# A six-stage transformer kernel: the second attention's weight split, border writes and norms are done at other places

## The chip, the cores and the metric

The kernel runs on one core of a Trainium2 chip. The core has five engines with a queue of instructions each: TensorE (PE), VectorE (DVE), ScalarE (ACT), GpSimd (POOL) and SyncE (SP, which here only issues DMAs). They run beside each other and wait for each other through semaphores. The metric is the device time of one execution in microseconds (us).

## The reference

The input x has 8 sequences of 256 tokens with 128 features (2048 rows). Six blocks follow each other, each on a layer norm of x and each added to x. The change concerns the fifth:

```python
x = x + 0.5 * _L0_ffn_ref(_layernorm(x), ...)    # f0: 64 experts, top 8
x = x + _L0_attn_ref(_layernorm(x), ...)         # a0
x = x + 0.5 * _L0_ffn_ref(_layernorm(x), ...)    # g0
x = x + 0.5 * _L1_ffn_ref(_layernorm(x), ...)    # f1: 8 experts, top 2
x = x + _L1_attn_ref(_layernorm(x), ...)         # a1
x = x + 0.5 * _L1_ffn_ref(_layernorm(x), ...)    # g1

# _L1_attn_ref: 16 heads of 64, causal, with a relative bias that depends on the query
Q = X @ Wq + bq;  K = X @ Wk;  V = X @ Wv        # 128 -> 16*64
R = X @ Wr + br                                  # 128 -> 16*10
extra[h,t,p] = sum_n R[h,t,n] * b_nd[n, t-p]     # only where p <= t
logits = Q K^T / 8 + extra, masked;  W = softmax(logits)
out = (W V) @ Wproj + bproj
```

## The kernel before, in words

Six stages f0, a0, g0, f1, a1, g1 run one after the other. Each is a set of five programs, one for each engine, written out by hand; what an engine does next is the order of its own program, and no scheduler changes it. At the end of a stage every engine passes a common barrier (`stage_end`), so nothing of a1 starts before f1 is done. x stays in SBUF from the first stage to the last.

**Stage a1 (`attention_one`)** works on a sequence (batch) at a time. Its products need more precision than one pass gives, so each operand is cut into a high part and a rest (`high_part`, `rest_part`) and a product is three matmuls (`matmul_by_parts`, lines 211 to 213). A batch's products come in 21 *pieces*, each of which fills one PSUM bank and is copied out by DVE or ACT (`store_piece`; those with odd number by ACT):

- R: X@Wr for both halves of the heads, six matmuls; DVE adds the bias and writes `RT`.
- G0 to G7: `RT` times the bias table `bnd`, one matmul each, of 40 partitions by 512 (in the trace two records each). The copy goes to `G`.
- QK0 to QK7: the transposed Q and K of two heads, six matmuls.
- V0 to V3: three matmuls of 512 columns.

G is written to a DRAM buffer `z` in rows three spans wide, whose two outer spans hold a large constant; read back with a stride one shorter than a row (line 1836, to `X0`, `X1`), it comes out shifted row by row: the bias by key, with the mask in place. Four pieces of G make half of a batch's heads (`c` is 0 or 1): two DMAs write them, and once these have landed two DMAs read them back.

**The start of a1 before the change.** DVE takes the statistics of all 16 tiles of 128 rows, then normalises them one by one (line 161, `a_xn`); PE turns each (line 167) into banks 0 to 3, and ACT copies each bank to `a_xnT` (line 180). Meanwhile SP loads the raw weights (lines 1795 to 1807), into the space of `X1[0]`, and then writes the borders of `z` from a tile `pad` with six DMAs (line 1814). After `a_xnT` ACT makes the high parts of the weights (line 2040), DVE the rests (line 202), and DVE then adds `bproj` to all of x (line 2093). POOL waits for all of `a_xnT` and then splits the first two batches' columns (`split`, lines 197 and 202, tiles `a_xs_high`, `a_xs_rest`). Only when DVE is through (`pe.wait_ge(prep, 2)`, `pe.wait_ge(w_rest, 4)`) does PE begin the first batch's pieces. They alternate between banks 5 and 6, in the order of the table `STEPS`:

```python
STEPS = ([("R", 0), ("QK", 0)], [("G", 0), ("G", 1), ("QK", 1)], [("G", 2), ("G", 3), ("QK", 2)], ...
```

A piece waits until its bank has been read, and a step's pair of G waits for both banks. Only after all 21 pieces does the main loop begin: 64 steps of two heads, scores (line 1932), logits on DVE (2107, 2109), exponentials on ACT (2049, 2051), normalising (1869, 1870), turning (1944), values (1964), with the next batch's pieces in between, and the projection (1974). In the loop POOL only splits later batches.

**Stage f1 (`mixture_one`)** is the one ahead. Its POOL program sends 32 groups of rows to their experts' slots by indirect DMAs (line 378); PE waits for them and for the gathered rows (line 347), and then does 39 passes (434, 444, 453). DVE has by then added the output bias (569) and copied the first three passes' weights (589).

## Time and profile before

| | us |
|---|---|
| median of 3 runs | 1273.78 (1270.94 to 1274.09) |
| profiled execution: its own time | 1271.9 |
| profiled execution: span, first to last instruction | 1269.9 |
| stage a1, first DVE instruction to g1's | 741.73 to about 1098 |
| in it: start of the first scores on PE | 792.00 |
| PE busy, of the span | 988.7 (78%) |
| DVE busy, of the span | 820.0 (65%) |
| POOL busy, of the span | 276.7 (22%) |

The times in the profile are microseconds from the first instruction. A busy share over the whole span says little here, as the six stages have different limits; the stage's own stretch is to be read. [...]

### The profile page before, as it was taken

To read this page: it belongs to the slowest core of one execution; us is meant where nothing else is said; L and a number is where in the kernel's file an instruction comes from. 1 tells how busy PE (TensorE), PEld (TensorE's weight loads), DVE (VectorE), ACT (ScalarE), POOL (GpSimd) and SP (SyncE) were. 2 spreads that over 40 slices of the span, in tenths; PEclk is the share of its full clock that TensorE was granted. 3 is DMA by queue.
4 is the path that set the end of the run, shared out by engine and by line. 5 is a ranking of instruction groups with operands and counts; after the bars stand their busy time and mean duration, and the time that the engine had idled before them with its cause. 6 is when DMAs were issued, how large, how long until landed. Compare 5 with 4: busy or idle time off the path is not lost.

```text
span 1269.9 us, 25097 instructions
## 1 busy us (share of the span) xinstructions
PE 988.7 (78%) x7978; PEld 739.0 (58%) x7978; DVE 820.0 (65%) x2678; ACT 572.9 (45%) x1503; POOL 276.7 (22%) x313
## 2 busy tenths in 40 slices
PE   4599867999996599894299717899999999634992
PEld 3256755666764255683179714566677666522992
DVE  5875887477876875787235482767776767570554
ACT  3103552356564102472045412777777777511551
POOL 2201136223201201202734410000000000055552
PEclk9799885589998699896599956999999999856997
DMA  8004000000006103009140178544345542464113
GB/s 226 1 0 114 0 15 0 1 1 2 1 2 160 34 0 100 13 1 227 52 107 29 29 256 241 164 120 135 116 133 167 143 123 68 77 174 118 33 32 105
DMA packets 131421, 105.39 MB, mean 83 GB/s; under 512 B 7987, under 2 KB 118107, under 8 KB 131316
## 3 DMA queue, kind: packets, MB, share of 16 engines
q1 hardware_dynamic: 126772, 95.55, 27.3%
q0 software_dynamic: 4544, 8.54, 2.1%
q8 instruction: 55, 0.90, 0.3%
q14 instruction: 50, 0.41, 0.1%
HBM read 66.14 MB, written 38.83 MB: 83 GB/s over the span
## 4 chain that ended last, share of the span: by engine, by line
PE 57%; DVE 22%; issue 8%; POOL 5%; ACT 3%; DMA 2%; DVEq 1%; POOLq 0%; SPq 0%; PEld 0%; ACTq 0%; PEldq 0%
PE psum L823 6%; PE psum L444 5%; PE psum L908 5%; PE psum L453 4%; PE psum L1433 3%; PE psum L211 3%; PE psum L1932 3%; PE psum L1482 3%; PE psum L1944 2%; PE psum L1974 2%; POOL f_slots_dram L378 2%; POOL g_slots_dram L378 2%; PE psum L1964 2%; PE psum L167 2%; PE psum L895 2%
## 5 line engine op out<-in xcount | busy, mean ns | idle before, releaser
L1613 DVE TENSOR_REDUCE a_negmax<-psum 128x2 f32<-128x512 f32 x128 | 84.9, 688 | 44.3 <-PE psum L1433 43.5
L1050 DVE TENSOR_TENSOR g_S<-g_place,g_number 128x512 bf16<-128x512 f32 (+1 forms) x116 | 76.8, 703 | 16.4 <-PEq L818 6.0
L1562 ACT ACTIVATE a_PT<-psum 128x1024 f32<-128x1024 f32 x64 | 65.4, 1022 | 34.9 <-PE psum L1465 34.6
L482 ACT ACTIVATE f_hT<-psum,f_tile_bias 128x128 f32<-128x128 f32 x156 | 44.5, 368 | 77.0 <-PE psum L444 77.0
L482 ACT ACTIVATE g_hT<-psum,g_tile_bias 128x128 f32<-128x128 f32 x156 | 44.5, 368 | 73.6 <-PE psum L444 73.6
L1050 DVE TENSOR_TENSOR f_S<-f_place,f_number 128x512 bf16<-128x512 f32 (+1 forms) x100 | 66.2, 704 | 14.9 <-PEq L818 6.2
L2049 ACT ACTIVATE a_pr<-a_L,a_least 128x128 f32<-128x128 f32 x128 | 50.8, 397 | 54.4 <-DVE a_least L2109 54.4
L1433 PE MATMUL psum<-a_turned 24*128 24x256 f32 x256 | 63.5, 377 | 5.7 <-DVE a_negmax L1613 5.6
L2051 ACT ACTIVATE a_pr<-a_L,a_least 128x256 f32<-128x256 f32 x128 | 63.6, 497 | 0.0
L1932 PE MATMUL psum<-a_KT,a_Q 64*128 64x128 f32 (+1 forms) x512 | 59.3, 350 | 1.4 <-DVE a_least L2109 1.4
L1459 PE MATMUL psum<-a_turned 24*128 24x256 f32 x256 | 57.3, 370 | 0.0
L2059 ACT ACTIVATE a_PT<-psum 128x384 f32<-128x384 f32 x128 | 55.6, 490 | 1.7 <-PE psum L1944 1.6
L1433 PEld LDWEIGHTS psum<-a_turned 24*128 24x128 f32 x256 | 42.6, 220 | 22.5 <-DVE a_negmax L1613 11.2
L1964 PE MATMUL psum<-a_PT,a_V 128*64 128x256 f32 (+1 forms) x512 | 55.5, 339 | 0.0
L1944 PE MATMUL psum<-ident,a_pr 128*128 128x128 f32 x384 | 52.9, 274 | 2.8 <-DVE a_pr L1870 2.5
L1964 PEld LDWEIGHTS psum<-a_PT,a_V 128*64 128x64 f32 x512 | 31.1, 136 | 40.9 <-issue 16.8
L197 POOL CAST a_xs_high<-a_xnT 128x256 fp32r<-128x256 f32 x8 | 4.3, 540 | 228.8 <-PE psum L213 219.0
L2109 DVE CUSTOM_DVE_ANT_0 a_L<-psum,a_X 128x256 f32<-128x256 f32 x128 | 53.8, 420 | 0.0
L384 POOL DMA_INDIRECT g_back_dram<-g_y,g_xin x39 | 43.3, 1109 | 43.7 <-DVE g_y L583 41.2
L589 DVE COPY f_wt<-f_w 128x1024 f32 x39 | 29.2, 749 | 35.9 <-PE psum L453 25.9
L384 POOL DMA_INDIRECT f_back_dram<-f_y,f_xin x39 | 40.8, 1047 | 48.8 <-DVE f_y L583 47.1
L589 DVE COPY g_wt<-g_w 128x1024 f32 x39 | 27.9, 720 | 34.9 <-PE psum L453 31.4
(527 smaller groups left out, 2875.9 us busy)
## 6 DMA issues: line engine op xcount, KB each, us to landing
a_z<-a_G SPq DMA_DIRECT2D x32, 512.0 KB, 3.2
a_X<-a_z SPq DMA_DIRECT2D x16, 1024.0 KB, 7.2
a_X<-a_z SPq DMA_DIRECT2D x16, 512.0 KB, 3.9
f_wgu<-in_gate_up SPq DMA_DIRECT2D x16, 384.0 KB, 6.6
...
a_z<-a_pad SPq DMA_DIRECT2D x6, 1024.0 KB, 8.6
...
```

The source lines that it names most:

```text
L384: pool.indirect_dma_start(back_dram[:, :], bass.IndirectOffsetOnAxis(ap=xin[:, i, P:P + 1].bitcast(I32), axis=0), y[i % YBUF][:, :], None, ...
L444: last = pe.matmul(bank[i % 2][:, P * c:P * c + P], wt[i % WBUF][:, P * c:P * c + P], xT[:, i % 2, :], start=True, stop=True)
L482: act.activation(hT[:, i % 2, c, :], bank[i % 2][:, P * c:P * c + P], ACT.Relu, bias=tile_bias[:, c, i:i + 1]).then_inc(relu_done, 1)
L823: pe.matmul(bank[k], xpart[:, i, ds(t, 1), :].rearrange("p t n -> p (t n)"), S[:, k, :], start=False, stop=False, skip_group_check=True)
L1050: return dve.tensor_tensor(S[:, slot, :].rearrange("p (t e n) -> p t e n", t=1, n=CAPACITY), bcast(place[:, ds(t, 1), CE * k:CE * k + CE], ...
L1433: last = pe.matmul(bank[h % 2][:, SEQ * t:SEQ * t + SEQ], q[rows, g, P * t:P * t + P].bitcast(F32R), k[rows, g, :].bitcast(F32R), start=Tr ...
L1562: act.activation(PT[m % 4][:, :, :, :].rearrange("p j t n -> p j (t n)"), core.psum[:, 2 + 2 * (u % 2):4 + 2 * (u % 2), :], ACT.Exp, scale ...
L1613: dve.tensor_reduce(negmax[:, :, h], bank[h % 2].rearrange("p (t n) -> p t n", n=SEQ), AX.X, ALU.max, negate=True).then_inc(max_done, 1)
L1932: last = pe.matmul(out, Q[s][rows, c, queries], KT[s][rows, c, keys], start=True, stop=True)
L1944: last = pe.transpose(bank[2 + i][:, P * j:P * j + P], pr[:, n % SLOTS, P * j:P * j + P], core.ident[:, :])
L1964: last = pe.matmul(o[D1 * i:D1 * i + D1, queries], V[s][:, kt, D1 * h:D1 * h + D1], PT[:, (2 * m + i) % TSLOTS, keys], start=(kt == 0), st ...
L2051: act.activation(pr[:, o, P:3 * P], L[:, o, P:3 * P], ACT.Exp, bias=least[:, o, 1:2], scale=-1.0, accum_out=sums[:, o, 1:2]).then_inc(p_re ...
```

## The change

- A new class `Early` holds a1's weights in high and rest parts, its bias tables and `z`. Its loads (SP), zero fills (POOL), high parts (ACT) and rests (DVE) are issued in stage f1: the loads behind f1's own weights, the fills at the head of POOL's program, the high parts ahead of f1's first relu, the rests between line 569 and line 589 of before. The raw weights have their own space.
- `pad` is filled at the head of a0 on POOL, and the six border DMAs are issued by SP in a0.
- In a1 DVE normalises only the first quarter (4 tiles); POOL does the other three. PE turns the first quarter, and the other three in between the first batch's pieces; ACT takes them likewise.
- The first batch's pieces use banks 5, 6, 7 and 4 in turn, in a new order, `FIRST`. Later batches are as before.
- `bproj` is added to x by POOL, a batch at a time, behind `split`; DVE's add of the projection waits for it.

```diff
+class Early:
+    def wait_split(self, eng):
+        eng.wait_ge(self.loaded, self.LOADS * 16)
+        eng.wait_ge(self.w_rest, len(self.cuts))
+        eng.wait_ge(self.prepared, 1)
+    def gpsimd(self, pool):
+        for m in (self.bnd[:, :, :], self.br[:, :], *(m[:, :, :, :] for m in self.wr)):
+            pool.memset(m, 0.0).then_inc(self.zeroed, 1)
+    def sync(self, sp):
...
+        for raw, m in zip(self.raw, ("Wq", "Wk", "Wv")):
+            sp.dma_start(raw[:, :], w[m]).then_inc(self.loaded, 16)
...
+    def scalar(self, act):
+        act.wait_ge(self.loaded, self.LOADS * 16)
+        act.wait_ge(self.zeroed, 4)
+        for raw, parts in self.cuts:
+            high_part(lambda out, in_: act.activation(out, in_, ACT.Copy), parts[0], raw).then_inc(self.w_high, 1)
+    def vector(self, dve):
+        dve.wait_ge(self.loaded, self.LOADS * 16)
+        dve.tensor_scalar(self.bq[:, 1, :], ...).then_inc(self.prepared, 1)
+        for i, (raw, parts) in enumerate(self.cuts):
+            dve.wait_ge(self.w_high, i + 1)
+            rest_part(dve, parts[1], raw, parts[0]).then_inc(self.w_rest, 1)
 def attention_one(core, name, ctx, w):
+    PIECE_BANKS = (5, 6, 7, 4)
+    FIRST = ([("R", 0)] + [("G", j) for j in range(4)] + [("QK", 0), ("QK", 1)] + [("G", j) for j in range(4, 8)]
+             + [("QK", 2), ("V", 0), ("V", 1), ("V", 2), ("V", 3)] + [("QK", j) for j in range(3, 8)])
     def gpsimd(pool):
-        pool.wait_ge(ln.xnT_ready, 4)
+        pool.wait_ge(ln.xn_ready, 4)
+        ln.normalise(pool, 1)
         split(0)
         split(1)
+        ln.normalise(pool, 2)
+        ln.normalise(pool, 3)
+        pool.wait_ge(early.prepared, 1)
+        add_bias(0)
+        add_bias(1)
         for b in range(BATCH):
             if b + 2 < BATCH:
                 split(b + 2)
+                add_bias(b + 2)
     def tensor(pe):
-        ln.tensor(pe)
-        pe.wait_ge(loaded, LOADS * 16)
-        pe.wait_ge(ln.xnT_ready, 4)
+        ln.turn_quarter(pe, 0)
+        early.wait_split(pe)
...
-        pe.wait_ge(prep, 2)
-        pe.wait_ge(w_rest, 4)
-        for u in range(len(STEPS)):
-            tables(0, u)
-            projections(0, u)
+        pe.wait_ge(zeroed, 1)
+        for n, k in enumerate(FIRST):
+            piece(0, k)
+            if n in (5, 8, 12):
+                ln.turn_quarter(pe, (5, 8, 12).index(n) + 1)
     def vector(dve):
-        ln.vector(dve)
-        dve.wait_ge(loaded, LOADS * 16)
-        dve.tensor_scalar(bq[:, 1, :], bq[:, 0, :], -RSCALE, None, ALU.mult).then_inc(prep, 1)
-        for i, (raw, parts) in enumerate(cuts):
-            dve.wait_ge(w_high, i + 1)
-            rest_part(dve, parts[1], raw, parts[0]).then_inc(w_rest, 1)
-        dve.wait_ge(ln.xn_ready, TILES)
-        dve.tensor_tensor(core.x[:, :, :], core.x[:, :, :],
-                          bp_row[:, :].unsqueeze(1).to_broadcast([P, TILES, P]), ALU.add).then_inc(prep, 1)
+        ln.statistics(dve)
+        ln.normalise(dve, 0)
```

PE at the start of a1, before the change: all 16 tiles are turned, then R (its six matmuls are two rounds of the first three rows), QK0 (`wq`, `wk`) and the first pair of G (`a_bnd,a_RT`), after which the same seven rows come again for QK1 and G2, G3, and so on.

```order
L167 MATMUL psum<-ident,a_xn 128x128 x16
L211 MATMUL psum<-a_xs_high,a_wr_rest 104x256
L212 MATMUL psum<-a_xs_rest,a_wr_high 104x256
L213 MATMUL psum<-a_xs_high,a_wr_high 104x256
...
L211 MATMUL psum<-a_xs_high,a_wq_rest 128x256
L212 MATMUL psum<-a_xs_rest,a_wq_high 128x256
L213 MATMUL psum<-a_xs_high,a_wq_high 128x256
L211 MATMUL psum<-a_xs_high,a_wk_rest 128x256
L212 MATMUL psum<-a_xs_rest,a_wk_high 128x256
L213 MATMUL psum<-a_xs_high,a_wk_high 128x256
L1896 MATMUL psum<-a_bnd,a_RT 128x512 x2
```

PE at the same place now (other line numbers; `early_` names the tiles of the new class):

```order
L278 MATMUL psum<-ident,a_xn 128x128 x4
L322 MATMUL psum<-a_xs_high,early_wr_rest 104x256
L323 MATMUL psum<-a_xs_rest,early_wr_high 104x256
L324 MATMUL psum<-a_xs_high,early_wr_high 104x256
...
L1985 MATMUL psum<-early_bnd,a_RT 128x512 x4
L322 MATMUL psum<-a_xs_high,early_wq_rest 128x256
L323 MATMUL psum<-a_xs_rest,early_wq_high 128x256
L324 MATMUL psum<-a_xs_high,early_wq_high 128x256
L322 MATMUL psum<-a_xs_high,early_wk_rest 128x256
L323 MATMUL psum<-a_xs_rest,early_wk_high 128x256
L324 MATMUL psum<-a_xs_high,early_wk_high 128x256
L278 MATMUL psum<-ident,a_xn 128x128 x4
```

Twelve of the sixteen turned tiles have moved from ahead of R to between the pieces, and four matmuls of G stand together in front of QK0.

DVE from the norms of a1 to its first piece, before:

```order
L161 TENSOR_SCALAR a_xn<-x,a_mean_var,a_rstd 128x128 x16
L2087 TENSOR_SCALAR a_bq<-a_bq 128x8
L202 TENSOR_TENSOR a_wr_rest<-a_X_0,a_wr_high 128x4x40
L202 TENSOR_TENSOR a_wq_rest<-a_X_0,a_wq_high 128x1024
L202 TENSOR_TENSOR a_wk_rest<-a_X_0,a_wk_high 128x1024
L202 TENSOR_TENSOR a_wv_rest<-a_X_0,a_wv_high 128x1024
L2093 TENSOR_TENSOR x<-x,a_bp_row 128x2048
L2010 TENSOR_SCALAR a_RT<-psum,a_br 104x256 x2
```

DVE there now:

```order
L272 TENSOR_SCALAR a_xn<-x,a_mean_var,a_rstd 128x128 x4
L2105 TENSOR_SCALAR a_RT<-psum,early_br 104x256 x2
L2113 COPY a_G<-psum 128x512 x2
L2118 TENSOR_SCALAR a_Q<-psum,early_bq 128x256
L2119 COPY a_KT<-psum 128x256
```

POOL there now, where before it had only the pairs of lines 197 and 202:

```order
L272 TENSOR_SCALAR a_xn<-x,a_mean_var,a_rstd 128x128 x4
L308 CAST a_xs_high<-a_xnT 128x256
L313 TENSOR_TENSOR a_xs_rest<-a_xnT,a_xs_high 128x256
L308 CAST a_xs_high<-a_xnT 128x256
L313 TENSOR_TENSOR a_xs_rest<-a_xnT,a_xs_high 128x256
L272 TENSOR_SCALAR a_xn<-x,a_mean_var,a_rstd 128x128 x8
L1936 TENSOR_TENSOR x<-x,early_bp_row 128x256 x2
```

Between the norms of the first quarter and R, DVE has lost five instructions; the norms of the second quarter now stand ahead of POOL's first split.

## Rows read from the trace of the kernel before

**Rows 1.** Windows: busy us and instructions of each engine, PEclk, DMA share, GB/s

```profile
748.00:752.50 4.50, 4.23 (x16) 2.90 (x16) 3.93 (x16) 1.79 (x4) 0.00 (x0) 0.50 0.98 268
763.80:783.70 19.90, 13.26 (x34) 6.20 (x34) 4.40 (x8) 3.88 (x8) 0.00 (x0) 0.50 0.81 237
783.70:787.20 3.50, 3.49 (x15) 3.25 (x15) 0.82 (x2) 0.52 (x2) 0.00 (x0) 0.55 0.67 201
787.20:792.00 4.80, 4.60 (x24) 3.07 (x22) 2.20 (x4) 1.57 (x4) 0.00 (x0) 1.00 0.92 282
```

**Rows 2.** Timeline, start of a1: start us, length us, engine, instruction, idle before

```profile
747.74 4.19 DVE L161 TENSOR_SCALAR a_xn<-x,a_mean_var,a_rstd 128x128 f32<-128x128 f32 x16
...
756.78 1.74 DVE L202 TENSOR_TENSOR a_wv_rest<-a_X,a_wv_high 128x1024 fp32r<-128x1024 f32 x1
758.44 2.28 DVE L2093 TENSOR_TENSOR x<-x,a_bp_row 128x2048 f32<-128x2048 f32 x1
...
760.93 0.51 PE L211 MATMUL psum<-a_xs_high,a_wr_rest 128*104 128x256 f32 x1 [8.47 <-DVE x L2093]
```

**Rows 3.** POOL: line 1325 (ns, min/median/max), and timeline of the first split

```profile
L1325 POOL TENSOR_SCALAR a_diag<-ident,a_wl x3: 597/597/598, 183.6 to 184.8; 128x128 f32<-128x128 f32 x3
...
753.16 0.40 POOL L197 CAST a_xs_high<-a_xnT 128x256 fp32r<-128x256 f32 x1 [9.79 <-ACT a_xnT L180]
753.64 0.72 POOL L202 TENSOR_TENSOR a_xs_rest<-a_xnT,a_xs_high 128x256 fp32r<-128x256 f32 x1
```

**Rows 4.** Timeline, first batch's pieces on PE, with DVE's copy of R

```profile
762.31 0.42 PE L211 MATMUL psum<-a_xs_high,a_wq_rest 128*128 128x256 f32 x1
...
762.62 0.88 DVE L2010 TENSOR_SCALAR a_RT<-psum,a_br 104x256 f32<-104x256 f32 x2 [1.90 <-PE psum L213]
...
763.38 0.42 PE L213 MATMUL psum<-a_xs_high,a_wk_high 128*128 128x256 f32 x1
...
764.75 2.08 PE L1896 MATMUL psum<-a_bnd,a_RT 40*128 40x512 f32 x4 [0.96 <-DVE a_KT L2024]
...
786.44 0.59 PE L211 MATMUL psum<-a_wv_high,a_xs_rest 128*128 128x512 f32 x1
786.87 0.40 PE L212 MATMUL psum<-a_wv_rest,a_xs_high 128*128 128x512 f32 x1
...
792.00 0.93 PE L1932 MATMUL psum<-a_KT,a_Q 64*128 64x128 f32 x8
...
795.76 1.13 PE L1896 MATMUL psum<-a_bnd,a_RT 40*128 40x512 f32 x4 [0.39 <-DVE a_KT L2024]
```

**Rows 5.** Windows and timeline: another rise of PEclk, and a long low stretch

```profile
204.00:260.00 56.00, 52.95 (x266) 38.10 (x267) 28.18 (x53) 16.18 (x22) 14.20 (x17) 0.50 0.00 1
...
1104.15 4.09 PE L167 MATMUL psum<-ident,g_rows 128*128 128x128 f32 x16 [7.09 <-DVE g_rows L161]
...
1107.00:1108.50 1.50, 1.50 (x11) 1.17 (x10) 0.85 (x4) 0.82 (x2) 0.00 (x0) 0.76 1.23 226
```

**Rows 6.** Lines of ACT, 741 to 793: busy us, mean ns, idle before

```profile
L2005 ACT ACTIVATE a_G<-psum 128x512 f32<-128x512 f32 x4 | 2.4, 597 | 20.1 <-PE psum L1896 20.1
```

**Rows 7.** DMA of 740 to 800: KB each, median us to landing

```profile
a_z<-a_G SPq DMA_DIRECT2D x5, 512.0 KB, 2.9
a_X<-a_z SPq DMA_DIRECT2D x2, 1024.0 KB, 6.8
```

**Rows 8.** Timeline of f1: DVE's weight copies, POOL's scatter, DVE's next work

```profile
608.99 0.97 POOL L378 DMA_INDIRECT f_slots_dram<-f_rows,f_slot  x1 [0.30 <-issue]
...
609.96 2.19 DVE L589 COPY f_wt<-f_w 128x1024 f32 x3
610.26 1.27 POOL L378 DMA_INDIRECT f_slots_dram<-f_rows,f_slot  x1 [0.30 <-issue]
611.84 1.16 POOL L378 DMA_INDIRECT f_slots_dram<-f_rows,f_slot  x1 [0.30 <-issue]
...
641.32 0.49 DVE L577 COPY f_xT<-psum 128x128 f32<-128x128 f32 x2 [29.17 <-PE psum L434]
```

More of the change, by code:

```diff
@@ L35 @@
 FC1 = F1 // P
+H1, D1, NB1, SPAN = 16, 64, 10, 128
+CH = H1 // 2
+RH = 8
+ZW = 3 * SPAN
+MASKED = 1e9
 class Chain:
@@ L138, in vector, with statistics @@
     def vector(self, dve):
+        self.statistics(dve)
+        for q in range(4):
+            self.normalise(dve, q)
+    def statistics(self, dve):
         c = Chain(self.chain)
@@ L159, in vector, with normalise @@
         step(dve.tensor_tensor(rstd, rstd, t, ALU.mult))
-        for t in range(TILES):
-            dve.tensor_scalar(self.xn[:, t, :], x[:, t, :], self.mean_var[:, t, 0:1], self.rstd[:, t:t + 1],
+    def normalise(self, eng, q):
+        x = self.core.x
+        for t in range(4 * q, 4 * q + 4):
+            eng.tensor_scalar(self.xn[:, t, :], x[:, t, :], self.mean_var[:, t, 0:1], self.rstd[:, t:t + 1],
                               ALU.subtract, ALU.mult).then_inc(self.xn_ready, 1)
@@ L329, in mixture_one @@
     back_loaded = [sem(f"back_loaded{i}") for i in range(4)]
+    early = core.early if name == "f1" else None
     def sync(sp):
@@ L355, in gpsimd @@
     def gpsimd(pool):
+        if early:
+            early.gpsimd(pool)
         pool.memset(empty[:, 0:P], 0.0).then_inc(empty_filled, 1)
@@ L1753, in attention_one @@
     piece_done = core.sem(f"{name}_piece_done")
-    piece_read = [core.sem(f"{name}_piece_read{i}") for i in range(2)]
+    piece_read = [core.sem(f"{name}_piece_read{i}") for i in range(len(PIECE_BANKS))]
     z_written = [core.sem(f"{name}_z_written{c}") for c in range(2)]
@@ L1880, in piece @@
             _, i, used = at(b, kind)
-            out = bank[5 + i]
+            out = bank[PIECE_BANKS[i]]
             if which == "R":
@@ L1925, in scores @@
             wait_piece(pe, b, "QK", c)
+            if not n:
+                pe.wait_ge(ln.xnT_ready, 4)
             if n:
@@ L2067, in take_values @@
             act.activation(AT[:, c, :], bank[4 + 3 * (c % 2)][:, 0:SEQ], ACT.Copy).then_inc(aT_ready, 1)
-        for u in range(len(STEPS)):
-            pieces_stored(act, True, 0, u)
+        for n, k in enumerate(FIRST):
+            if by_act(k):
+                store_piece(act, True, 0, k)
+            if n in (6, 10, 14):
+                ln.take_quarter(act, (6, 10, 14).index(n) + 1)
         for n in range(BATCH * CH + VLAG):
@@ L2122, in add @@
             dve.wait_ge(out_done, b + 1)
+            dve.wait_ge(x_biased, b + 1)
             xb = core.x[:, 2 * b:2 * b + 2, :]
             dve.tensor_tensor(xb, xb, bank[7][:, 0:SEQ].rearrange("p (t n) -> p t n", n=P), ALU.add).then_inc(out_added, 1)
-        for u in range(len(STEPS)):
-            pieces_stored(dve, False, 0, u)
+        for k in FIRST:
+            if not by_act(k):
+                store_piece(dve, False, 0, k)
         for n in range(BATCH * CH):
@@ L2149, in build @@
         stage_done = core.sem("stage_done")
+        core.early = Early(core)
         made, sems, held = [], [], []
@@ L2163, in build @@
         out_dram = out.rearrange("(t p) d -> p t d", p=P)
+        names = [name for name, _ in stages]
         def stage_end(eng, n):
@@ L2174, in _ @@
                 st["sync"](sp)
+                if names[n] == "a0":
+                    core.early.write_pads(sp)
                 if n:
@@ L2185, in _ @@
             for n, st in enumerate(made):
+                if names[n] == "a0":
+                    core.early.fill_pad(pool)
                 st["gpsimd"](pool)
```

169 lines of the change are left out of this document (99 added, 70 removed).

## The prediction

> **What bounds the kernel now.** The stages stand behind barriers, so I read only the stage that is changed and the two that take over its work. First the windows by stage part [rows 1]: from 748.0 to 792.0 the granted clock is 0.50 until 787 and PE is busy for two thirds of it. The reader is to see that this stretch, ahead of the first scores at 792.00 [rows 4], has no engine that is full. Then the timeline of the stage's start [rows 2]: R, the first piece, begins at 760.93 and had waited 8.47 us for DVE, which was splitting weights and adding bproj from 752 to 760.7. Third the timeline of the pieces [rows 4]: from 760.93 to 792.00 are 31.1 us, in which PE works at the lower clock and pauses at each pair of G (0.96 us ahead of the first), because two banks must both be read. The rest of a1 is a loop of 64 steps whose instructions the change leaves as they are, but for POOL's adds.
>
> **The start of the stage.** DVE's four norms of the first quarter end at 747.74 + 4.19/4 = 748.8 [rows 2]. R now needs, on POOL, four norms, the cast (0.40) and the rest (0.72 with a gap of 0.08) [rows 3]. The trace has no norm on POOL. The nearest row is a tensor_scalar of the same 128x128 with one factor, 0.597 us; a norm has two. Bounds: 0.40, the cast of twice the size, and 0.72, the two-input operation of twice the size [rows 3]; so four cost 1.6 to 2.9 us. I take 4 x 0.60 = 2.4. Then 748.8 + 2.4 + 1.2 = 752.4, and with 0.1 for the signal R starts at 752.5. That is 8.4 us earlier than 760.93. The first quarter's turning and its copy on ACT run beside POOL's norms: they were going at 749.4 to 750.0 before too, ahead of 751.2.
>
> POOL's other splits and norms: second split until 753.6, eight norms until 758.4, each well ahead of the turning that needs it (below: 760.6 at the earliest). The two first bias adds, about 0.7 us each, follow; the remaining six lie in the loop, in which POOL had only the splits. Their consumer on DVE is a whole batch later. I cost them at nothing; if DVE's SBUF work is held up by them, 8 x 0.7 = 5.6 us is the most it could cost in 300 us of loop, and DVE has pauses there.
>
> [...]
>
> **The pieces.** Durations at the lower clock [rows 4]: R 762.31 - 760.93 = 1.4; QK five steps in 1.07, so six matmuls 1.28; a pair of G 2.08, so 1.04 each; V 3 x 0.43 = 1.29. A quarter's turning is 4.23/4 = 1.06 [rows 1]. A pair of G takes 1.13 at the full clock [rows 4], a factor of 0.54, which I use for all.
> - R from 752.5 to 753.9. G0 waits for DVE's copy of R: 763.50 + 0.1 against 762.31, a gap of 1.3. G0 starts at 755.2.
> - From there PE has, all at the lower clock, 8 x 1.04 (G) + 8 x 1.28 (QK) + 4 x 1.29 (V) + 3 x 1.06 (turning) = 8.3 + 10.2 + 5.2 + 3.2 = 26.9 us of work.
> - No more waits: a bank comes round after three other pieces, at least 1.7 us even at the full clock, and a copy is 0.60 on ACT for G [rows 6], 0.9 for QK, each engine having only half of them (some 8 us on DVE, 10 us on ACT with its three quarters). What hides them is PE's own queue; with two banks again it would be the pauses of [rows 4].
> - When does the clock rise? In the trace it rose at 786.85 (0.55 in a window of 3.5 us is a tenth of it at 1.00), 3.1 us into the first stretch without a pause and without G [rows 1], and at 1107.7, 3.6 us into 16 turned tiles [rows 5]. It did not rise in 16 tiles at 748.2 to 752.5, nor in the 19.9 us in which G and QK took turns [rows 1], nor from 204 to 260, where PE was busy for 53 of 56 us with matmuls of which most use 24 partitions [rows 5]. In the new order matmuls of G (40 partitions) stand at 755.2 to 759.4, and again, with turning between, at 763.0 to 768.2. From there on, QK2, V and QK3 to QK7, all have 128 partitions. I put the rise 3.4 us (mean of 3.1 and 3.6) behind 768.2, at 771.6.
> - Until then 16.4 of the 26.9 us are done; the other 10.5 take 10.5 x 0.54 = 5.7. First scores at 777.3 instead of 792.0: 14.7 us earlier, 8.4 of them from the start, 6.3 from pauses and clock.
> - Late next are the X tiles, which DVE's first logits need. G3 ends at 759.4, its copy at 760.2; write 2.9, two reads with the larger 6.8 us after its issue [rows 7], about 1 for issuing: 770.9. This is 6 us ahead of need. SP has no longer the borders to write in front of them.
> - ACT loads its exponential table only behind the copy of QK7, which is now the last piece; before it was V3. I add 0.2.
>
> **Borders in a0.** Six writes of 1 MB and one small fill of POOL. The DMAs stand behind a0's loads on SP, whose program there ends with them; a0 ran with idle DMA (share 0.00 [rows 5]). Nothing waits but SP. Cost 0, at most 0.3 for the fill.
>
> **Split in f1.** Loads of 2.2 MB behind f1's weights, ACT 3.5 us ahead of the first relu, DVE three rests of at most 1.74 [rows 2] and a small one of 0.4, 5.6 us at most and about 4.9 as the longest had POOL beside it, behind the bias additions. DVE is then idle for 29.17 us until 641 [rows 8], as POOL scatters rows; it hides DVE and ACT. But POOL's scatter is what ends last there. Beside DVE's 2.19 us of weight copies two of its instructions took 1.27 and 1.16 instead of 0.97 us [rows 8], a loss of 0.5. The new 4.9 us of DVE could cost between 0 and 0.5 x 4.9/2.2 = 1.1; I take 0.7. [...] POOL's four fills at the head, 1.4 us, delay the emptying of the slots, with 5 us to spare.
>
> **Sum.** -14.7 + 0.2 + 0.7 = -13.8 us. On the profiled execution's own time of 1271.9: 1258.1. The median of the three runs is 1.9 above that execution, the lowest 1.0 below; I add 0.9, half of it: 1259.
>
> **The rivals.**
> - *The clock rises in the first dense stretch.* For it: from 755.2 PE has no pause at all, which it never had before. Against: 4.2 of the first 7.8 us are G. With the rise at 759 to 763, 3.8 to 7.8 us are done low, and the scores start at 771.7 to 773.5, the X tiles being there at 770.9. That is 4 to 5.5 us better, 1254. [...]
> - *It does not rise before the scores.* Scores at 755.2 + 26.9 = 782.1, a gain of 9.9, less 0.9: 1263, or 1264 with the half offset. POOL's norms at their upper bound would add 0.5.
> - *Slower: the low clock goes on into the loop.* Now the loop has always run at 1.00, as the last pieces raised it. A long low spell in a busy PE exists, 56 us in a0 [rows 5]. The loop's PE is busy to about nine tenths; the same 56 us at a factor 0.54 to 0.6 would lose 22 to 25 us against a gain of 9: 1286. It decides from about 20 us of low loop on. Against it: 13.9 us of matmuls of 128 partitions stand directly ahead of the loop, where 3.1 and 3.6 were enough.
> - *The gain is not there because something is waited for elsewhere*: POOL's scatter slowed more, or the X tiles late by the traffic of f1 or a0. Price 3 to 8 us: 1262 to 1267.
>
> **Chances.** Forecast 0.50, early rise 0.26, no rise before the scores 0.13, low loop 0.04, held up elsewhere 0.07. The range from 1250 to 1267 takes in all but the low loop, and bounds for POOL's norms and the runs' own spread of 3 us. 0.3% is 3.8 us, about what a measurement of this kernel can tell from no change: only the slow loop is above 1277.6, and a part of the last case could be within. Faster 0.93, same 0.03, slower 0.04.
>
> **What would show it.** R's first matmul 11 us behind the stage's first DVE instruction, not 19; POOL's norms near 0.6 us; no pause above 0.3 us on PE between G0 and the scores; PEclk 0.50 while G stands between, 1.00 from 16 us behind G0; first scores 35.6 us into the stage (50.3 before). In f1, the stretch of the scatter longer by under 1.1 us. It is wrong if the pauses remain, if DVE's first logits wait for a DMA, or if the loop takes longer than before.

## The result

| | before | after |
|---|---|---|
| median, us | 1273.93 (4 runs, 1270.94 to 1274.53) | 1256.20 (4 runs, 1252.07 to 1260.92) |
| profiled execution: time, span | 1271.9, 1269.9 | 1252.09, 1250.3 |
| stage a1 in it | 355.9 | 339.5 |
| R behind the stage's start | 19.2 | 11.68 |
| first scores behind the stage's start | 50.27 | 32.15 |
| first scores to g1 | 305.7 | 307.3 |
| the five other stages | 906.5 | 903.4 |

The ratio is 0.9883, with a 95% interval of 0.9844 to 0.9922: 1.2% faster. The same kernel, run again in more rounds as the experiment `again`, had 1258.02 (6 runs, 1241.21 to 1260.18) and 0.9854 [0.9802, 0.9905]. Ratios are taken from fast runs alone, and two of these six count as slow (1260.18, which is the profiled one, and 1259.84), so the ratio isn't that of the two medians. Stage times are taken from one stage's first statistics instruction on DVE to the next one's. Of the 19.6 us by which the two profiled spans differ, 16.4 are a1. The other 3.1 can't be put down to the change: a0 took 213.7 us before and 202.8 after, f0 and g0 each 4 us more, and later kernels show 202 or 211 to 214 us for a0 with the same code, by how long its low clock lasts (from 204 until 238 in `after`, from 196 until 261 in `before`).

The windows of the changed kernel, start of a1 (busy us and count of PE, PE's weight loads, DVE, ACT and POOL, then PEclk, the granted clock of TensorE as a share of its full speed, DMA share, GB/s); they answer to [rows 1]:

```profile
752.80:756.60 3.80, 3.71 (x8) 1.18 (x8) 0.73 (x2) 0.60 (x1) 3.80 (x6) 0.50 0.00 0
756.60:760.20 3.60, 3.60 (x18) 3.49 (x16) 1.50 (x3) 0.60 (x1) 2.37 (x4) 0.50 0.97 290
760.20:763.10 2.90, 2.90 (x13) 1.12 (x12) 0.69 (x1) 1.80 (x4) 0.00 (x0) 0.94 0.13 23
763.10:770.80 7.70, 7.70 (x54) 6.98 (x52) 4.19 (x9) 4.27 (x9) 0.00 (x0) 1.00 1.05 318
777.50:781.50 4.00, 3.93 (x22) 3.55 (x24) 1.35 (x7) 2.85 (x9) 0.00 (x0) 0.57 0.50 153
```

PE is full from G0 (752.89) to the scores. The clock is back at 1.00 at about 760.6, 7.7 us behind G0 and not 16 us. The last window is new: some us into the loop the clock falls again, for 3.4 us (0.57 over 4 us); before, the whole loop ran at 1.00.

The timeline of the changed kernel, rows that answer to [rows 2 to 4] (start us, length us, engine, instruction, idle before):

```profile
744.68 1.11 DVE L272 TENSOR_SCALAR a_xn<-x,a_mean_var,a_rstd 128x128 f32<-128x128 f32 x4
745.90 3.14 POOL L272 TENSOR_SCALAR a_xn<-x,a_mean_var,a_rstd 128x128 f32<-128x128 f32 x4 [6.74 <-DVE a_xn L272]
749.00 0.39 POOL L308 CAST a_xs_high<-a_xnT 128x256 fp32r<-128x256 f32 x1
749.48 0.72 POOL L313 TENSOR_TENSOR a_xs_rest<-a_xnT,a_xs_high 128x256 fp32r<-128x256 f32 x1
750.35 0.51 PE L322 MATMUL psum<-a_xs_high,early_wr_rest 128*104 128x256 f32 x1 [4.03 <-POOL a_xs_rest L313]
...
770.82 0.93 PE L2024 MATMUL psum<-a_KT,a_Q 64*128 64x128 f32 x8
771.78 0.29 DVE L2192 CUSTOM_DVE_ANT_0 a_L<-psum,a_X 128x128 f32<-128x128 f32 x1 [0.74 <-PE psum L2024]
...
774.59 1.13 PE L1985 MATMUL psum<-early_bnd,a_RT 40*128 40x512 f32 x4 [0.39 <-DVE a_KT L2119]
777.57 0.54 PE L322 MATMUL psum<-a_xs_high,early_wq_rest 128*128 128x256 f32 x1 [1.85 <-DVE a_G L2113]
```

R waits for POOL now, for 4.03 us where it waited 8.47 for DVE. A norm on POOL is 0.785 us (3.14/4). The first logits wait for PE, not for a DMA. The pause of 1.85 us behind the first G of the loop stood in the kernel before as well, without a fall of the clock.

f1 in the changed kernel, DVE and POOL; it answers to [rows 8]:

```profile
626.31 0.69 DVE L688 TENSOR_TENSOR x<-x,psum 128x512 f32<-128x512 f32 x1 [10.52 <-remote]
...
627.22 1.22 DVE L313 TENSOR_TENSOR early_wq_rest<-early_raw_wq,early_wq_high 128x1024 fp32r<-128x1024 f32 x1
628.06 1.23 POOL L495 DMA_INDIRECT f_slots_dram<-f_rows,f_slot  x1 [0.30 <-issue]
...
629.59 1.97 POOL L495 DMA_INDIRECT f_slots_dram<-f_rows,f_slot  x1 [0.30 <-issue]
630.63 2.04 DVE L710 COPY f_wt<-f_w 128x1024 f32 x3
631.86 1.05 POOL L495 DMA_INDIRECT f_slots_dram<-f_rows,f_slot  x1 [0.30 <-issue]
```

The scatter's instructions lengthen from 0.97 to 1.23, 1.97 and 1.05 us beside DVE's rests and copies. From its first to its last it takes 41.31 us (595.74 to 637.05), before 40.54. DVE's last bias addition came at 626.31; before it was at 609.21. This returns below.

### The profile page after: what moved, and what is told of

The parts are those of the page before. It is cut to its first block, busy times and chain, and to the rows that moved or that the text cites. A ratio compares the mean times of both kernels' runs of the same rounds, so it can differ in the third digit from the quotient of the medians.

```text
span 1250.3 us, 25112 instructions
## 1 busy us (share of the span) xinstructions
PE 982.0 (79%) x7978; PEld 738.3 (59%) x7978; DVE 812.6 (65%) x2665; ACT 573.8 (46%) x1503; POOL 296.7 (24%) x333
## 4 chain that ended last, share of the span: by engine, by line
PE 56%; DVE 21%; issue 11%; SPq 5%; ACT 3%; DMA 2%; POOL 2%; DVEq 0%; PEld 0%; POOLq 0%; ACTq 0%; PEldq 0%
PE psum L561 6%; PE psum L944 6%; PE psum L570 5%; PE psum L1029 5%; PE psum L1554 3%; PE psum L1603 3%; PE psum L322 2%; PE psum L2024 2%; PE psum L2069 2%; PE psum L2036 2%; DVE a_L L2194 2%; PE psum L1016 2%; SPq L454 1%; PE psum L324 1%; PE psum L323 1%
## 5 line engine op out<-in xcount | busy, mean ns | idle before, releaser
L1554 PE MATMUL psum<-a_turned 24*128 24x256 f32 x256 | 59.6, 355 | 6.6 <-DVE a_negmax L1734 6.4
L501 POOL DMA_INDIRECT f_back_dram<-f_y,f_xin x39 | 44.8, 1148 | 41.0 <-DVE f_y L704 40.0
L1580 PE MATMUL psum<-a_turned 24*128 24x256 f32 x256 | 53.0, 349 | 0.0
L1554 PEld LDWEIGHTS psum<-a_turned 24*128 24x128 f32 x256 | 39.3, 203 | 21.8 <-DVE a_negmax L1734 11.0
```

The costliest lines, as they stand in the source:

```text
L501: pool.indirect_dma_start(back_dram[:, :], bass.IndirectOffsetOnAxis(ap=xin[:, i, P:P + 1].bitcast(I32), axis=0), y[i % YBUF][:, :], None, ...
L1554: last = pe.matmul(bank[h % 2][:, SEQ * t:SEQ * t + SEQ], q[rows, g, P * t:P * t + P].bitcast(F32R), k[rows, g, :].bitcast(F32R), start=Tr ...
```

## The experiments

Lengths in us from each profile. "Low in the loop" is the time at 0.50 behind the first scores, from the granted clock. Where no count of runs stands, it is one run (four for `before` and `after`); the kernel before, timed beside them, had medians of 1271.1, 1274.5, 1275.4 and 1271.1.

| run | time | R | scores | scores to g1 | a1 | low in the loop | f1 |
|---|---|---|---|---|---|---|---|
| before | 1273.93 | 19.2 | 50.27 | 305.7 | 355.9 | 0 | 170.2 |
| after | 1256.20 | 11.68 | 32.15 | 307.3 | 339.5 | 3.4 | 170.2 |
| again | 1258.02 (6) | 11.67 | 31.63 | 311.8 | 343.4 | 17.1 | 167.5 |
| g_first | 1259.39 | 11.67 | 35.19 | 308.1 | 343.3 | 6.8 | 167.7 |
| two_banks | 1255.23 | 11.67 | 41.5 | 307.2 | 348.7 | 3.4 | 170.5 |
| split_late | 1264.64 | 16.29 | 37.09 | 307.2 | 344.3 | 3.4 | 168.0 |
| quarter_dve | 1250.44 (5) | 9.70 | 29.65 | 311.7 | 341.4 | 17.1 | 170.1 |
| warm | 1254.53 | 11.67 | 31.16 | 307.1 | 338.2 | 3.4 | 167.4 |
| pads_late | 1258.38 | 11.67 | 31.79 | 312.7 | 344.5 | 10.2 | 167.1 |
| loop_fill | 1251.56 (4) | 11.67 | 31.58 | 305.8 | 337.4 | 0 | 167.5 |
| warm_rt | 1254.18 | 11.68 | 27.95 | 307.5 | 335.4 | 3.4 | 173.4 |
| both | 1259.92 (6) | 9.70 | 30.21 | 305.5 | 335.8 | 0 | 174.9 |
| everything | 1255.97 (6) | 9.70 | 26.58 | 305.8 | 332.4 | 0 | 177.0 |
| rests_last | 1249.07 (6) | 9.71 | 25.98 | 306.0 | 332.0 | 0 | 168.5 |

The time of a whole run carries some 10 us of other stages, so the verdicts go by the stage. Each rests on one profile of its kernel, and two profiles are compared where their loops were low for about the same time, as a1 alone differs by 3.9 us between the two profiles of the changed kernel.

**again.** The changed kernel, unaltered.

> The changed kernel once more, for a second profile and five more timings. Theory: a1 is shortened by the change in every execution, by 14 to 18 us from its first DVE instruction to g1's (355.9 us before, 339.5 in the first profile), and the scatter stretch of f1 is longer by about 0.8 us; the 8.5 us between the changed kernel's two pairs of times (1252.1, 1252.1, 1260.9, 1260.3) come from the length of low-clock spells in a0, f0 and g0, which the change does not touch (a0 took 213.7 us before and 202.8 after). Rival: a1 itself has two states, so that a profile of a slow execution shows a1 about 8 us longer. In figures: a1 338 to 342 us by the theory whatever the total, 346 to 350 in a slow execution by the rival.

The start repeats to 0.5 us. a1 is 343.4, and its windows show where the 4 us more are:

```profile
778.20:795.50 17.30, 15.76 (x65) 10.96 (x66) 9.13 (x41) 9.44 (x33) 0.00 (x0) 0.51 0.62 194
795.50:1080.00 284.50, 265.82 (x2115) 194.19 (x2114) 204.46 (x950) 213.87 (x762) 9.14 (x15) 1.00 0.41 121
```

The clock is low for 17.1 us of the loop instead of 3.4; from 795.5 on it is 1.00 as in `after`. So the fall behind the first scores costs 1.6 to 6.1 us against the 305.7 of before, from one run to the next; `quarter_dve` shows the 17.1 us too. The expectation is missed on both sides: 343.4 lies above the theory's 338 to 342 and below the rival's 346 to 350. The two profiled spans differ by 8.1 us. a0 makes 8.1 of them and a1 3.9, g1 2.3 and f0 0.3, while g0 and f1 are 4.1 and 2.7 shorter. So a1 has a part of its own in the spread, though not the whole of it.

**g_first.** All of G stands ahead of the QK pieces.

```diff
-    FIRST = ([("R", 0)] + [("G", j) for j in range(4)] + [("QK", 0), ("QK", 1)] + [("G", j) for j in range(4, 8)]
-             + [("QK", 2), ("V", 0), ("V", 1), ("V", 2), ("V", 3)] + [("QK", j) for j in range(3, 8)])
+    FIRST = ([("R", 0)] + [("G", j) for j in range(8)] + [("QK", 0), ("QK", 1), ("QK", 2)]
+             + [("V", 0), ("V", 1), ("V", 2), ("V", 3)] + [("QK", j) for j in range(3, 8)])
```

> All eight G pieces stand behind R, ahead of QK0. In the changed kernel the clock rose at about 22 us of the stage, 7.6 us behind G0's start and 3.9 us behind QK0's. Theory A: the 40-partition matmuls of G do nothing for the clock, it rises 3 to 5 us behind the first full-height piece; QK0 now starts at about 22 us, so the rise is at 25 to 27 us, and first scores at 33.5 to 35 us. Theory B: any stretch without a pause raises it, G too; then it rises by 22 us at the latest, within or just behind the eight G, and scores are at 31 to 32.5 us as in the changed kernel (32.15).

Its windows from G0 on:

```profile
754.30:765.20 10.90, 10.90 (x24) 4.42 (x25) 2.77 (x4) 2.88 (x5) 6.05 (x9) 0.50 0.34 98
765.20:767.50 2.30, 2.30 (x13) 2.30 (x12) 0.61 (x2) 0.00 (x0) 0.00 (x0) 0.52 0.93 230
767.50:775.00 7.50, 7.50 (x54) 6.92 (x54) 3.46 (x8) 4.42 (x10) 0.00 (x0) 1.00 0.89 278
```

PE is full for 10.9 us with G and two turnings, and the clock stays at 0.50; it rises 2.2 us behind the first QK matmul. In the changed kernel it rose 4.0 us behind QK0. That is theory A in kind: the rise came 27.3 us into the stage and the scores at 35.19, both 0.2 to 0.3 us past its ranges, as it had left out the two turnings (1.1 us each) among the eight G. So the prediction's reading that G's matmuls do not raise the clock holds in this profile; what was wrong was to make the rise wait for the end of the last G.

**two_banks.** The first batch's pieces in banks 5 and 6 alone, in the new order.

```diff
-            i = n % (len(PIECE_BANKS) if b == 0 else 2)
+            i = n % 2
...
-    first_reads = [len(range(i, len(FIRST), len(PIECE_BANKS))) for i in range(len(PIECE_BANKS))]
+    first_reads = [0] * len(PIECE_BANKS)
...
```

> The changed kernel with the first batch's pieces in two banks (5 and 6) in the new order. Theory: four banks removed PE's pauses, and by that brought the clock up early. With two banks pauses of about 0.7 us come back between the G pieces and of 0.3 to 0.5 us between the others, the clock rises late or not at all before the scores, and these come 27 to 30 us behind R instead of 20.5: at 39 to 42 us of the stage, a1 7 to 10 us longer. Rival: the earlier start and the order do it alone; then scores are at 33 to 35 us.

Its timeline on PE:

```profile
750.09 2.08 PE L1985 MATMUL psum<-early_bnd,a_RT 40*128 40x512 f32 x4 [0.78 <-DVE a_G L2110]
752.95 0.58 PE L322 MATMUL psum<-a_xs_high,early_wq_rest 128*128 128x256 f32 x1 [0.78 <-DVE a_G L2110]
...
763.47 0.58 PE L322 MATMUL psum<-a_xs_high,early_wq_rest 128*128 128x256 f32 x1 [0.78 <-DVE a_G L2110]
...
774.53 0.93 PE L2024 MATMUL psum<-a_KT,a_Q 64*128 64x128 f32 x8
```

The pauses are back, the clock rises only at 768.3, 21.1 us behind G0 instead of 7.7, and the scores come 9.3 us later than in the changed kernel, 29.8 us behind R against 31.1 before. All of this is as the theory had it. The four banks are the larger half of the gain: they take away the pauses and the longer part of the low clock.

**split_late.** All of `Early`'s work (loads, fills, high parts, rests) is issued in a1 again, the raw weights lying in X1[0]; the borders stay in a0.

```diff
-        if early:
-            early.sync(sp)
...
-        if early:
-            early.gpsimd(pool)
...
-        if early:
-            early.scalar(act)
...
-        if early:
-            early.vector(dve)
...
     def sync(sp):
+        early.sync(sp)
...
     def gpsimd(pool):
+        early.gpsimd(pool)
...
         ln.take_quarter(act, 0)
+        early.scalar(act)
...
         ln.statistics(dve)
         ln.normalise(dve, 0)
+        early.vector(dve)
```

> The weights' loads, zero fills, high parts and rests are back in a1 (f1 as before), all else as changed. Theory: R waits for DVE's last rest, which needs the last load (11 us into the stage before), the high parts and four rests; R at 16 to 17 us instead of 11.7, and scores 4 to 5 us later than 32.15, at 36 to 37.5; f1's scatter stretch is again 42.9 us instead of 43.7. So of the 18 us that the scores moved the split is worth 4 to 5, net of f1 about 4. Rival: POOL's four norms are what R waits for, and the split costs R under 2 us.

POOL and PE in its timeline:

```profile
759.68 5.43 POOL L271 TENSOR_SCALAR a_xn<-x,a_mean_var,a_rstd 128x128 f32<-128x128 f32 x3
...
763.15 0.51 PE L321 MATMUL psum<-a_xs_high,early_wr_rest 128*104 128x256 f32 x1 [8.64 <-DVE early_wv_rest L312]
```

R waits for DVE's rests, 4.6 us later, and a1 loses 4.8 us (to `after`; the two loops are alike). Beside the rests three POOL norms took 5.43 us, 1.81 each against 0.785 with DVE idle. In f1 the scatter was 40.10 us long against 41.31 to 41.78 in `after`, `again` and `g_first`: the early split costs it 1.2 to 1.7, loads included.

**quarter_dve.** DVE takes the norms of quarter 1 back; POOL starts with the splits.

```diff
     def gpsimd(pool):
-        pool.wait_ge(ln.xn_ready, 4)
-        ln.normalise(pool, 1)
         split(0)
         split(1)
+        pool.wait_ge(ln.xn_ready, 8)
         ln.normalise(pool, 2)
...
         ln.normalise(dve, 0)
+        ln.normalise(dve, 1)
```

> The norms of quarter 1 go back to DVE, which was idle there (it waited 6.17 us for PE in the changed kernel); POOL begins with the splits and does quarters 2 and 3 behind them. Theory (POOL's four norms of 0.785 us each stand on the chain between DVE's first four norms and R): DVE's second four take 1.1 us instead of 3.1, so R begins 9.6 to 9.9 us into the stage instead of 11.67, first scores at 29.5 to 30.5 us instead of 31.6 to 32.2, a1 1.5 to 2.5 us shorter, some 1254 against the changed kernel's 1256 to 1258. Rival (the chain goes through ACT's transfers or PE's turning of quarter 0, which has the same end whoever makes quarter 1; or the clock's rise, which is fixed, gives it back): R at about 11.5, or R at 9.7 but scores still at 31.6 or later, and the time unchanged.

R at 9.70 and scores at 29.65: 2.0 us each, as the theory had it. DVE does four norms in 1.1 us where POOL takes 3.14, and it was idle. Its a1 is still 341.4, because the loop had 17.1 us of low clock; against `again`, with as much, it is 2.0 shorter. Median 1250.44 (5 runs, 1249.07 to 1252.65; 1254 was expected), ratio 0.982 [0.9803, 0.9837].

**warm and warm_rt.** Idle matmuls, whose results nothing reads, between turning quarter 0 and R; in `warm_rt` four more between R and G0 (the second part of the code).

```diff
         early.wait_split(pe)
+        for _ in range(9):
+            pe.matmul(bank[3], core.ones[:, :], core.tri[:, :].unsqueeze(1).to_broadcast([P, 4, P]), start=True, stop=True)
...
         for n, k in enumerate(FIRST):
             piece(0, k)
+            if n == 0:
+                for _ in range(4):
+                    pe.matmul(bank[3], core.ones[:, :], core.tri[:, :].unsqueeze(1).to_broadcast([P, 4, P]), start=True, stop=True)
```

> Nine idle matmuls of 128 x 512 in bf16, whose results nothing reads, are put on PE between turning quarter 0 and R, in the wait of 4 us for POOL; bank 3 is free there. Theory (what G, QK and R lose is the clock, which rises some us after PE has had full-size work to do without a pause): the clock is at 1.00 before or soon after R begins at 11.7 us into the stage, the 7.6 us of low clock behind G0's start go, and the first scores come at 27.5 to 29.5 us into the stage instead of 31.6 to 32.2. Rival (the rise depends on something else than PE's own work, such as a phase that runs on from stage to stage): the clock rises at the same distance from the stage's start as before, 22 us, and the scores come at 31.6 to 32.2, or later by what the idle matmuls delay R.

> As in the run warm (nine idle matmuls ahead of R), and four more of them between R and G0, where PE waits 0.97 us for DVE to write RT. In warm the clock rose 2.9 us behind the first idle matmul (753.2), stayed at 1.00 through R and fell again at 756.7, just behind the start of G0, 0.3 us after PE had stood for 0.97 us. Theory (the pause between R and G lets it fall): the clock stays at 1.00 through G and QK0, the eight records of G take some 2.1 us instead of 3.6 to 3.8, and the scores come 3 to 4.5 us earlier than in warm (31.16), at 26.7 to 28.2 us into the stage. Rival (G itself lets it fall, or what is short is not this pause): 0.50 again within 2 us of G0's start, scores at 31 or more.

Windows of `warm`:

```profile
753.25:756.50 3.25, 1.64 (x11) 0.93 (x9) 0.88 (x2) 0.00 (x0) 3.08 (x6) 1.00 0.00 0
756.75:760.00 3.25, 3.25 (x9) 0.78 (x5) 0.69 (x2) 0.60 (x1) 3.25 (x5) 0.50 0.00 1
```

Timeline of `warm_rt` on PE:

```profile
752.36 4.00 PE L1966 MATMUL psum<-tri,ones 128*128 128x512 bf16 x9
756.60 0.34 PE L322 MATMUL psum<-a_xs_high,early_wr_rest 128*104 128x256 f32 x1 [0.23 <-POOL a_xs_rest L313]
...
757.36 1.04 PE L2080 MATMUL psum<-tri,ones 128*128 128x512 bf16 x4
758.49 1.99 PE L1987 MATMUL psum<-early_bnd,a_RT 40*128 40x512 f32 x8
```

In `warm` the clock rose 3.0 us behind the first idle matmul (750.29 to 753.25), 10.4 us into the stage and not 22 as the rival had it, so here it followed PE's own work. R had the higher clock, and it fell 0.3 us behind the start of G0, after pauses of 0.65 us ahead of R and 0.97 behind it. Scores at 31.16 are only 0.5 us better than in `again`; 27.5 to 29.5 had been expected. In `warm_rt` the second pause is filled (and the first was 0.23): all of G ran at 1.00, G0 to G3 in 1.99 us instead of 3.78, and the scores came 3.2 us earlier than in `warm`, within what was expected. So G did not make the risen clock fall here. The pauses ahead of it are what differs: the clock fell in the one profile with both, and stayed in the three in which the second was filled (`warm_rt`, `everything`, `rests_last`). Which of the two matters isn't shown.

**pads_late.** `pad` filled and the borders written at the start of a1.

```diff
     def sync(sp):
+        core.early.write_pads(sp)
...
-                if names[n] == "a0":
-                    core.early.write_pads(sp)
...
-                if names[n] == "a0":
+                if names[n] == "a1":
                     core.early.fill_pad(pool)
```

> The tile pad is filled and the borders of z written (six DMAs) at the start of the second attention, as in the kernel before, instead of the first; all else as in the changed kernel. Theory (the borders cost nothing in the first attention and little in the second, because the X reads are not waited for): scores stay at 31.6 to 32.2 us, the reads of X are issued up to 10 us later than now (23 us into the stage), the first logits on DVE, now 33.1 us into the stage, wait by 0 to 4 us, a1 0 to 4 us longer. Rival (the border writes are what the change gained by): a1 longer by more than 6 us with the first logits at over 39 us. In the first attention the removal changes nothing by either, beyond the two lengths (202 and 211 to 214 us) that it shows with any kernel.

DMA issues in its timeline:

```profile
738.23 17.22 SPq L131 DMA_DIRECT2D z<-pad  x6
763.16 1.01 SPq L1908 DMA_DIRECT2D z<-a_G  x2
767.61 0.99 SPq L1918 DMA_DIRECT2D a_X<-z  x2
```

The first logits on DVE, same timeline:

```profile
775.50 0.29 DVE L2193 CUSTOM_DVE_ANT_0 a_L<-psum,a_X 128x128 f32<-128x128 f32 x1 [5.52 <-DMA a_X<-z]
```

The first write of G waits for the borders, X is read 29.6 us into the stage (23.0 in the changed kernel), and DVE's first logits wait for it until 37.5 instead of 33.1, 4.4 us later where the theory had at most 4. a1 is 344.5, with 10.2 us of low clock in the loop, which is more than `after` had and less than `again`. An estimate parts the two: loops with 3.4, 6.8 and 17.1 us of low clock were 1.6, 2.4 and 6.1 us longer than before, so 10.2 us would cost some 3.7 of the 7.0 by which this loop is longer, and the wait some 3.3. The write in a0 saves up to 4.4 us, the lateness of the first logits; it gains nothing by itself, but without it the early scores would not be usable. In the kernel before it was hidden.

**loop_fill.** Eight idle matmuls in the pause of 1.85 us in the loop's second step.

```diff
                 tables(b + 1, u)
+            if n == 1:
+                for _ in range(8):
+                    pe.matmul(bank[3], core.ones[:, :], core.tri[:, :].unsqueeze(1).to_broadcast([P, 4, P]), start=True, stop=True)
```

> Eight idle matmuls of 128 x 512 in bf16 go into bank 3, which is free there, in the loop's second step between G of the next batch and QK, where PE of the changed kernel pauses 1.85 us for DVE's copy of G; after this pause its clock was at 0.50 for 3.7 us (and for 18 us in the run again, whose loop took 311.8 us instead of 307.3). Theory (the pause behind a pair of G is what lets the clock fall): no stretch of 0.50 in the loop, loop 305.7 us from the first scores to the next stage, as in the kernel before, a1 1.5 us shorter and the time 1 to 4 us less. Rival (the clock falls for another reason, or falls at another pause): a stretch of 0.50 is still there behind step 2, loop 307 or more, time unchanged.

Its window of the loop's start:

```profile
769.60:785.00 15.40, 13.85 (x97) 8.65 (x96) 12.20 (x60) 11.36 (x38) 1.82 (x3) 1.00 0.62 192
```

Its timeline on PE, the idle matmuls and what follows them:

```profile
774.44 1.90 PE L2086 MATMUL psum<-tri,ones 128*128 128x512 bf16 x8
776.36 0.39 PE L322 MATMUL psum<-a_xs_high,early_wq_rest 128*128 128x256 f32 x1
```

No low clock, and 305.8 us for the loop, as before and as the theory had it. Of the thirteen profiles of kernels with the change, the four with this fill have no low stretch in the loop and the nine without it all have one.

**both and everything.** `both` is `quarter_dve` with `loop_fill`; `everything` adds five idle matmuls ahead of R and four behind it.

> quarter_dve and loop_fill in one kernel. If their two gains add up: R at 9.7 us into the stage, scores at 29.65, loop 305.8, a1 335.4 us (against 339.5 and 343.4 in the two runs of the changed kernel), and the median some 1246 to 1248, against 1250.44 and 1251.56 with one of them each. Rival (the clock only falls at another place of the loop when the stage is shifted by 2 us): a stretch of 0.50 behind the first scores again, loop 307 to 312, median 1250 or more.

> both, with five idle matmuls ahead of R and four between R and G0. If the clock can be raised ahead of R and kept: the 2.8 us that G, QK0 and their neighbours lose at low clock go, scores at 26 to 28 us into the stage, median 1243 to 1246. Rival (R comes too early for the clock, since it begins only 2 us behind the first idle matmul, or G lets it fall): scores at 29 to 30.5, median as of both or up to 1 us more, since the idle matmuls delay R.

In a1 the gains add up: 335.8 and 332.4 us. The medians do not show it (ratios 0.988 [0.9827, 0.9933] and 0.9855 [0.9802, 0.9907]): 1259.92 and 1255.97 where 1246 to 1248 and 1243 to 1246 were expected. In their profiles f1 took 174.9 and 177.0 us, and 173.4 in `warm_rt` beside them; g1 took 181.1 in `both`, against 171.6 in `loop_fill`. The code of f1 and g1 is the changed kernel's in all three. PE in f1 of `everything`:

```profile
603.67 7.19 PE L538 MATMUL psum<-f_b,f_exT 8*128 8x128 f32 x32 [2.10 <-DMA f_w<-in_W]
...
647.48 2.07 PE L561 MATMUL psum<-f_xT,f_wt 128*128 128x128 f32 x8 [6.81 <-DVE f_xT L698]
```

DVE there:

```profile
623.50 0.69 DVE L688 TENSOR_TENSOR x<-x,psum 128x512 f32<-128x512 f32 x1 [12.05 <-remote]
641.01 0.69 DVE L688 TENSOR_TENSOR x<-x,psum 128x512 f32<-128x512 f32 x1 [16.83 <-remote]
...
641.93 1.22 DVE L313 TENSOR_TENSOR early_wq_rest<-early_raw_wq,early_wq_high 128x1024 fp32r<-128x1024 f32 x1
...
645.33 1.89 DVE L710 COPY f_wt<-f_w 128x1024 f32 x3
647.14 0.49 DVE L698 COPY f_xT<-psum 128x128 f32<-128x128 f32 x2
```

By the profile PE has made the last product of the output bias at 610.9; DVE adds it at 641.01. "remote" says only that no instruction was found for the signal that released DVE. The trace has the time of the signal itself, the increment of the semaphore `b2_done` that goes with PE's product. For the fourth product, in us:

| profile, stage | product's end on PE | signal | DVE's addition |
|---|---|---|---|
| `rests_last`, f1 | 610.98 | 610.99 | 611.02 |
| `after`, f1 | 608.89 | 626.28 | 626.31 |
| `after`, g1 | 1113.71 | 1135.62 | 1135.64 |
| `warm_rt`, f1 | 612.17 | 641.06 | 641.08 |
| `warm_rt`, g1 | 1117.13 | 1124.50 | 1124.52 |
| `both`, f1 | 609.50 | 639.30 | 639.33 |
| `both`, g1 | 1120.97 | 1152.86 | 1152.88 |
| `everything`, f1 | 610.86 | 640.99 | 641.01 |
| `everything`, g1 | 1118.15 | 1136.57 | 1136.59 |

So DVE isn't held: it starts 0.02 us behind the signal, and the signal is late. In the ten other profiles it comes within 0.02 us of the product's end, in f1 and in g1; in these four it is late in both stages. A matmul's end is modelled in the profile, so whether PE's products or only their signals were late can't be told, and the cause stays open. In `both` f1 and g1 are together 16.9 us longer than in `loop_fill`, which is more than the 14.4 by which its span is longer. Whether the runs without a profile had late signals isn't known, so that they explain the medians isn't shown.

All that DVE has behind the additions in f1 is then late, and of the 6.81 us that PE waits at 647.48, 3.7 are the early rests (641.62 to 645.33). In `after` the fourth addition came at 626.31, where the slack to 641 still covered it.

**rests_last.** As `everything`, with the rests behind f1's last pass.

```diff
-        if early:
-            early.vector(dve)
         dve.wait_ge(experts_ready, 1)
...
         y_out(PASSES - 1)
+        if early:
+            early.vector(dve)
         dve.wait_ge(b2_added, 4)
```

> As everything, and DVE writes the rests of the second attention's weights (and scales bq) in the mixture ahead of it behind its last pass, where it waits 7.5 us for the gathered rows, instead of ahead of its copies of the first three passes' weights. In the traces of warm_rt, both and everything DVE's third and fourth addition of the output bias came at 623 to 641 us, up to 31 us behind the products that they read (PE was done at 610.9), and the first pass then waited 6.8 us for DVE, 3.7 us of which are the rests; in seven other traces of kernels with the early split the additions were done by 616 and the rests hid. Theory (the rests are then on the chain of the mixture, and behind its last pass they lie in a wait): if the additions are late again, the first pass's products wait 3 to 3.3 us instead of 6.8 and the mixture takes 3.5 us less than 177.0; if they are not late, they wait 0.3 us as before and the mixture's length stays at 167.5 to 170.5. In both cases DVE's wait for the gathered rows shrinks from 7.5 to 2.5 us, the second attention is 332.4 us, R at 9.7, scores at 26.6. Median 1243 to 1248, or 1251 to 1253 on a chip like that of everything. Rival (the rests delay the adding of the gathered rows, or R's wait for them, by more than they give): the mixture 1 to 5 us longer than 170.5 with the additions not late.

DVE at the end of f1:

```profile
723.04 1.21 DVE L313 TENSOR_TENSOR early_wk_rest<-early_raw_wk,early_wk_high 128x1024 fp32r<-128x1024 f32 x1
724.18 1.21 DVE L313 TENSOR_TENSOR early_wv_rest<-early_raw_wv,early_wv_high 128x1024 fp32r<-128x1024 f32 x1
729.53 9.36 DVE L729 SCALAR_TENSOR_TENSOR x<-f_back,f_weight,x 128x128 f32<-128x128 f32 x32 [4.15 <-DMA f_back<-f_back_dram]
```

The rests lie in a wait of which 4.15 us are left; f1 is 168.5, and a1 332.0, the shortest of all. The additions were not late in this profile, so what the new place saves when they are was not seen. Median 1249.07 with all six runs from 1248.06 to 1250.89, ratio 0.9839 [0.9806, 0.9872]. The expectation had 1243 to 1248, or 1251 to 1253 with late additions. This is the lowest median, but on another chip; by the ratio to the kernel before on the same chip it can't be told from `quarter_dve` (0.982), `loop_fill` (0.984) or `again` (0.9854), whose intervals it overlaps. By a1 it beats the changed kernel by 7.5 us or more, and the kernel before by 23.9.

## Why the prediction was right

Forecast 1259 with 1250 to 1267; 1256.2 and, again, 1258.0. Its steps:

- **Start of the stage.** R forecast 8.4 us earlier, measured 7.5. The norm on POOL was taken at 0.60, with 0.72 as the upper bound; it is 0.785. The bound was wrong: neither row was an operation with two factors per row. Four times 0.185 is 0.7 of the 0.9 us missing. Of the 7.5 us only a part is shown: 4.6 are the split (`split_late`); the other 2.9 (`bproj`, one quarter turned ahead of R instead of four, norms on two engines) were not undone one by one.
- **The pieces.** No pause between G0 and the scores: right. From R to the scores 24.8 us forecast, 20.5 measured. **The step that failed is the clock's rise**, put 3.4 us behind the end of G7 (16.4 us behind G0); it came 7.7 us behind G0, just behind the first two QK pieces and 0.2 us into G4. With the rise put there the prediction's own sum gives 7.7 + (26.9 - 7.7) x 0.54 = 18.1 us from G0 to the scores, and 17.9 were measured, so its costs and its factor hold. The premise that G doesn't raise the clock is borne out (`g_first`); the conclusion that G, standing in between, puts off the rise isn't. The rival of the early rise, given 0.26, happened, with scores 32.15 us into the stage where it said 30.0 to 31.8 and R came 0.9 late. But the length of the unbroken stretch alone did not decide it: in the changed kernel the rise came 7.7 us into it, in `g_first` PE was full for 10.9 us and the clock stayed at 0.50.
- **The loop.** Forecast unchanged. It was 1.6 us longer in `after` and 6.1 in `again`, which the prediction itself had named as a sign of being wrong: the slow rival in miniature, 3.4 to 17.1 us of low clock and not 56. The fall hangs on the pause at the second step (`loop_fill`); `before` has the same pause and no fall, and why is open. The 0.2 us for ACT's exponential table is about right: its load began 0.72 us behind the first scores in `before` and 0.88 in `after`.
- **f1.** The scatter longer by 0.77 in `after`, forecast 0.7; in `again` it was 1.24 longer (41.78 against 40.54), past the 1.1 given as the most. `split_late`, with no rests in f1, had 40.10. The forecast took the rests to cost as much per microsecond as DVE's copies [rows 8], which was an estimate. Measured beside the early rests and the copies was one scatter instruction of 1.97 us instead of 0.97 (`after`), and beside the rests a norm of 1.81 instead of 0.785 (`split_late`). Not foreseen: that the additions can come 30 us late, so that the 29 us of slack [rows 8] are not always there.
- **X tiles and borders.** X was read at 761.63 and 771.75, the first logits did not wait: right. Cost in a0 0: no run shows any.

So the near hit is partly a balance, and partly luck: on the two profiled executions the forecast was -13.8 us. a1 brought -16.4, of which -18.1 stand ahead of the scores (forecast -14.7) and +1.6 in the loop; the other stages brought -3.1 (a0 -10.8, f0 +3.9, g0 +4.0, f1 and g1 -0.1 each), which varies as much with the same code. In `again` a1 brought -12.5. The early rise gave more than was forecast, and the fall in the loop took 1.6 to 6.1 us of it back.

By the parts, undone one at a time, in one profile each (such parts need not add up): four banks 9.2 us of a1, the split in f1 4.8, the borders 3.3 to 4.4. The norms on POOL cost 2.0 against leaving one more quarter on DVE.
